# Stores as plain DMAs from SyncE, loads by a table of rows from GpSimd, and another map of partitions

## The reference

```python
g = group_norm(x, 32 groups of 12 channels, eps=1e-5)     # (g - mean) / sqrt(var + eps)
off_round = round(offset)                                 # 48 positions, 8 channels each
y = displace(g, off_round)                                # shift by (ox, oy), zeros come in
kern = exp(-(dx*dx + dy*dy) / (2 * 0.5**2)); kern /= sum  # 3x3 taps from offset - off_round
out = x + depthwise_conv3x3(y, kern)
```

## Time and profile before

| | |
|---|---|
| median of three runs | 976.11 us |
| profiled execution | 978.52 us, its span 976.7 us |
| VectorE busy | 871.0 us (89%) |
| ScalarE busy | 714.3 us (73%) |
| GpSimd busy | 326.6 us (33%) |
| TensorE busy | 201.4 us (21%) |
| bytes by DMA | 403.48 MB, mean 413 GB/s over the span |

### The profile page before, as it was taken

How to read it: one execution, slowest core, us unless ns; L and a number is a source line. 1 busy time by engine, 2 the same in 40 slices (tenths; PEclk the granted TensorE clock), 3 DMA queues, 4 the chain that set the end, 5 groups by cost and what they waited for, 6 DMA issues and landing times.

```text
span 976.7 us, 3636 instructions
## 1 busy us (share of the span) xinstructions
PE 201.4 (21%) x896; PEld 195.9 (20%) x896; DVE 871.0 (89%) x940; ACT 714.3 (73%) x412; POOL 326.6 (33%) x196
## 2 busy tenths in 40 slices
PE   0331312212122121222202212212122122220120
PEld 0331312212122121222202212212122122220120
DVE  5389899999999999799999999999999979679990
ACT  3998959777687686878777786868778787878720
POOL 3032352443514333142315263252522423224320
DMA  8999999999999999999999999999999999999996
GB/s 358 428 368 421 420 422 414 424 404 395 415 426 411 405 423 412 424 421 429 429 424 419 417 415 416 421 407 429 418 419 419 417 428 427 422 431 406 428 429 280
DMA packets 28233, 403.48 MB, mean 413 GB/s; under 512 B 3506, under 2 KB 3506, under 8 KB 3634
## 3 DMA queue, kind: packets, MB, share of 16 engines
q0 software_dynamic: 27648, 402.67, 99.0%
q1 hardware_dynamic: 562, 0.57, 0.2%
HBM read 201.90 MB, written 201.33 MB: 413 GB/s over the span
## 4 chain that ended last, share of the span: by engine, by line
DVE 48%; DMA 39%; issue 5%; ACT 4%; POOL 3%; POOLq 0%; ACTq 0%; DVEq 0%
DMA out<-tiles,row_of 30%; DVE tiles L437 17%; DVE rowblur L412 8%; DMA tiles<-x,row_of 8%; DVE tiles L439 8%; DVE rowblur L417 8%; DVE normed L396 5%; POOL tiles L187 3%; ACT unread L242 3%; ACT unread L246 1%; DVE scale L351 0%; DVE shift L354 0%; DVE var_p L341 0%; DVE apart L335 0%; DVE apart L337 0%
## 5 line engine op out<-in xcount | busy, mean ns | idle before, releaser
L242 ACT ACTIVATE unread<-tiles 128x4096 uint8<-128x4096 f32 x94 | 339.9, 3616 | 167.6 <-DMA tiles<-x,row_of 167.0
L246 ACT ACTIVATE unread<-tiles,nmean_p 128x4096 uint8<-128x4096 f32 x94 | 348.7, 3709 | 3.0
L187 POOL DMA_INDIRECT tiles<-x,row_of x96 | 156.8, 1633 | 518.0 <-DMA out<-tiles,row_of 512.6
L437 DVE SCALAR_TENSOR_TENSOR tiles<-rowblur,ratio,tiles 128x735 f32<-128x735 f32 (+24 forms) x192 | 300.0, 1562 | 4.6
L216 PE MATMUL mean_ps<-nmean_p,mask 128*128 128x1 f32 x448 | 100.7, 353 | 562.7 <-ACT unread L242 535.3
L216 PEld LDWEIGHTS mean_ps<-nmean_p,mask 128*128 128x128 f32 x448 | 98.0, 330 | 565.3 <-ACT unread L242 538.0
L192 POOL DMA_INDIRECT out<-tiles,row_of x96 | 169.7, 1768 | 109.6 <-DVE tiles L437 85.3
L412 DVE SCALAR_TENSOR_TENSOR rowblur<-normed,ratio 128x784 f32<-128x784 f32 (+14 forms) x96 | 152.2, 1586 | 3.4
L439 DVE TENSOR_TENSOR tiles<-rowblur,tiles 128x784 f32<-128x784 f32 (+14 forms) x96 | 146.5, 1526 | 3.3
L417 DVE SCALAR_TENSOR_TENSOR rowblur<-normed,ratio,rowblur 128x752 f32<-128x752 f32 (+14 forms) x96 | 145.5, 1515 | 3.4
L216 PE MATMUL var_ps<-var_p,mask 128*128 128x1 f32 x448 | 100.7, 354 | 174.6 <-DVE var_p L341 174.6
(11 more groups left out here) (34 smaller groups left out, 25.7 us busy)
## 6 DMA issues: line engine op xcount, KB each, us to landing
tiles<-x,row_of POOLq DMA_INDIRECT x96, 14.9
out<-tiles,row_of POOLq DMA_INDIRECT x96, 17.6
mask<-masks SPq DMA_DIRECT2D x1, 448.0 KB, 3.2
row_of<-rows SPq DMA_DIRECT2D x1, 48.0 KB, 1.8
offs<-offset SPq DMA_DIRECT2D x1, 48.0 KB
plan_sb<-planned SPq DMA_DIRECT2D x1, 0.4 KB
offs_p<-offset SPq DMA_DIRECT2D x1, 0.4 KB
steps_sb<-steps SPq DMA_DIRECT2D x1, 12.0 KB
```

The costliest lines, as they stand in the source:

```text
L187: pool.indirect_dma_start(tiles[:, n % SLOTS, :], None, x_rows, bass.IndirectOffsetOnAxis(ap=row_of[:, n:n + 1], axis=0)).then_inc(loaded[ ...
L242: nc.scalar.activation(unread[:], tiles[:, n % SLOTS, :], ACT.Identity, scale=-1.0 / HW, accum_out=nmean_p[:, i % 2, j:j + 1]).then_inc(nm ...
L246: nc.scalar.activation(unread[:], tiles[:, n % SLOTS, :], ACT.Square, bias=nmean_p[:, i % 2, j:j + 1], accum_out=m2_p[:, i % 2, j:j + 1]). ...
L437: ins = nc.vector.scalar_tensor_tensor(y, t, ratio[:, (tap + 1) // 2, p, 1:2], y, ALU.mult, ALU.add)
```

## The change

SyncE gets a loop over the 96 tiles: it waits for the last column tap of tile n and issues its store as a plain DMA, from the tile's 128 partitions to 16 images by 8 channels by one plane of `out`. GpSimd keeps only the loads: after the first ten, it waits for the store of tile n to have landed and issues load n + 10. A plain DMA needs a regular pattern of addresses, so the map of partitions becomes the regular one: partition p holds image p div 8 of the half batch, channel p mod 8 of the position. Before, eight partitions such as 0 to 3 and 32 to 35 held one channel of eight images (0, 2, 4 ... 14), and the next four partitions the next channel. Both host tables are made from the map and change with it. The rest of the program is the same.

```diff
@@ -76,7 +76,7 @@
 def image_of_partition():

     p = np.arange(128)
-    return 2 * (p // 32 % 2 * 4 + p % 4) + p // 64, p // 4 % CH
+    return p // CH, p % CH
@@ -89,7 +89,7 @@
-    out_rows = out.rearrange("b c y x -> (b c) (y x)")
+    out_images = out.rearrange("b c y x -> b c (y x)")
@@ -178,6 +178,12 @@
             sp.dma_start(mask[:], masks).then_inc(masks_in, 16)

+            for n in range(ALL):
+                at, p = n // TILES * BT, CH * ORDER[n]
+
+                sp.wait_ge(col_taps, 1 + (n + 1) * COL_TAPS)
+                sp.dma_start(out_images[at:at + BT, p:p + CH, :], tiles[:, n % SLOTS, :]).then_inc(stored[n % SLOTS], 16)
+
             for n in range(ALL - SLOTS, ALL):
                 sp.wait_ge(stored[n % SLOTS], landed(n))
@@ -188,21 +194,13 @@
-            def store(n):
-                pool.indirect_dma_start(out_rows, bass.IndirectOffsetOnAxis(ap=row_of[:, n:n + 1], axis=0),
-                                        tiles[:, n % SLOTS, :], None).then_inc(stored[n % SLOTS], 16)
-
             pool.wait_ge(rows_in, 16)
             for n in range(SLOTS):
                 load(n)
-            for n in range(ALL):
-
-                pool.wait_ge(col_taps, 1 + (n + 1) * COL_TAPS)
-                store(n)
-
-                if n and n - 1 + SLOTS < ALL:
-                    pool.wait_ge(stored[(n - 1) % SLOTS], landed(n - 1))
-                    load(n - 1 + SLOTS)
+            for n in range(ALL - SLOTS):
+
+                pool.wait_ge(stored[n % SLOTS], landed(n))
+                load(n + SLOTS)
```

## The result

The changed kernel takes 1025.25 us (median of four runs, 1019.32 to 1030.67), the kernel before 976.1 (four runs). The ratio is 1.0517, 95% interval 1.0478 to 1.0555, or +50 us. Forecast were 995 us in a range of 957 to 1042: the direction and the range held, the size was off by more than half. The profiled execution took 1027.41 us, its span 1025.6.

A forecast was written before the change was run, and what follows sets the result against it. Transfers bound the kernel: stores 503.3 us, loads and tables 483.0, edges 12.6, hole -2.5 make 996.4 against the span of 976.7, +19.7; on the median 995.8, forecast 995 us, range 957 to 1042.

The forecast's parts named there:

- The bound: Whole kernel: DMA transfers set the time, 403.48 MB at 418.5 GB/s plus 12.6 us lost at start and end.
- The disputed term: New partition map and plain store form: stores at 400 GB/s, loads at 418.5; with the other terms, +19.7 us.
- rival C: Stores: plain form uses engines or ports unevenly, stores at 368 GB/s, 1040 us in all; chance 0.11.
- Mixing or issuing: Mixed middle loses 28 us against one-way 936.2: loads and stores disturbing each other (preferred), or GpSimd's descriptor work.
- A: Mixed middle: GpSimd's issuing was the cost, so traffic runs at 427 GB/s; 962 us, at best 953; chance 0.31.
- The hole: At 60 to 75 us, late load 10 drops the rate to 348 GB/s; a separate store queue gains 2.5 us.
- SyncE's issues: On SyncE's queue: 96 plain DMAs at 0.42 us each, 40 us spread over 977; cost 0.
- TensorE: TensorE gets the same instructions as before; cost 0.
- stores on time: Mid-program: SyncE sends a store at 409.6, not 7.7 us late; the full DMA queue hides it, gain 0.

The follow-up runs named there:

- 32 x 4, near rows: Changed kernel, each store written as 32 blocks of 4 adjacent rows, 128 KB apart, so planes land in other places than wanted: 957.89 us, ratio 0.9793.
- the 1.5 MiB pitch: Changed kernel with each store as 128 x 4096 to rows 1.5 MiB apart, not the wanted places: 959.39 us, ratio 0.9818 to the kernel before.
- Loads of 16 x 8: Changed kernel with plain 16 x 8 x 4096 loads from GpSimd and plain stores of 128 adjacent rows, not the wanted places: 1085.04 and 1096.9 us.
- the run with 128 adjacent rows: Changed kernel, each plain store writing its 128 planes to 128 adjacent output rows, not the wanted places: 955.91 us, ratio 0.9793 to the kernel before.
- reads over 32 images: Changed kernel with tiles of 4 channels of 32 images, stores 32 x 4 x 4096: 1006.29 us; reading 128 adjacent rows instead: 983.42 us.

## Why the prediction was right and wrong, point by point

**The bound, right.** The transfers set the time before and after; the sum closes (482.0 + 535.4 us of packets in 1025.6).

**The disputed term, right in sign, wrong in size and in cause.** The step that failed is "I take the stores at 400 and the loads at 418.5". Loads: 418, as taken. Stores: 376. The 400 came from a mixed stretch of the kernel before, and no row of before held a store of this pattern; what the runs show in its place is the division of 16 x 8, which loses 6.5% by itself. Split up by the runs, the +5.2% are about

| | ratio to before |
|---|---|
| the map of partitions | +0.55% |
| stores as plain DMAs on SyncE, well divided (32 x 4, near rows), against the map alone | 0.9793/1.0055, -2.6% |
| division 16 x 8 instead of 32 x 4, both to near rows | 1.0432/0.9793, +6.5% |
| 16 x 8 to the right places instead of near rows | 1.0517/1.0432, +0.8% |

The intervals of the two ratios in the last step overlap, and the 1.5 MiB pitch cost 0.4%. One term of +6.5% hid a gain of 2.6%. My sum had neither; it knew of an unusual shape ("that DMA has a destination of 128 rows; the store's is 16 x 8 x 4096") and left that to rival C.

**Mixing or issuing, wrong.** I leaned to mixing, because loads alone ran at 427 under GpSimd's issues. With well divided plain stores the mixed middle runs at 431 and 425, and 952.8 - 12.6 = 940.2 us are left against the one-way 936.2: mixing costs 4 us at most, not 28. The other 24 went with the indirect stores. Which part of them it was, the form, the descriptors made by GpSimd, the order in one queue or the later issue, the runs do not tell apart. The issues of 1.04 and 2.67 us that the prediction set against each other do not help: one is a store, the other a load, and VectorE was at work beside both.

**The rivals A and C were both at work.** A priced 962 us, at best 953; the well divided stores gave 956 to 959. That the gain comes from issuing, as A had it, is open as said above. C overlaid it. C looked in the right place ("uses the engines or their ports unevenly"), at 1040 us and a chance of 0.11; that the stores are unevenly served is shown, that it is at the ports is inferred. Its price came near by luck: the 368 GB/s that it took is the slice of the hole in the kernel before, which has nothing to do with a store's division, and the stores happened to run at 376.

**The hole**, -2.5: it vanished in the rows, and cannot be seen in the time.

**Costs put at nothing**: SyncE's issues (0.54 us each, not 0.42) and TensorE, right. What stores on time are worth is part of the -2.6% and open. VectorE has 85% of the span (below 87% forecast), GpSimd 146.4 us (near 157), the middle 399 to 404 GB/s (below 415).

## What to carry to other kernels

A DMA's shape is part of its price: a transfer of 128 partitions written as 16 x 8 lost half the rate where only such transfers ran, and its stores a tenth beside good loads, while the same bytes as 32 x 4, 64 x 2 or 128 rows lost nothing. Before a store is moved to a plain DMA, look at the outermost size of its pattern, and choose the map of partitions so that it is 32 or more for 128 partitions; then count what that map does to the reads. When two suspected costs are of opposite sign, price each by itself: a near-zero or moderate sum says nothing about either.

## What the hardware showed that I had not expected

- Loads of 16 x 8 with nothing beside them: 217 GB/s, against 434 for the indirect loads, both with the DMA share at 1.01. A share of 1 says that engines hold packets, not that they move bytes.
- Loads and stores on the same engines at once reach 431 GB/s (300 to 700 us of the run with 128 adjacent rows: 431 and 425), as much as one direction alone.

```profile
300.00:500.00 200.00, 41.72 (x186) 40.51 (x186) 194.29 (x197) 153.77 (x90) 28.87 (x21) 1.00 1.01 431
500.00:700.00 200.00, 40.92 (x182) 39.80 (x182) 196.15 (x171) 150.37 (x86) 37.64 (x21) 1.00 1.01 425
```

- Writes hardly minded rows 1.5 MiB apart (959.39 against 955.91 us); reads over 32 images cost 23 us against adjacent rows, though loads alone ran at 436 GB/s there.
